# One program block instead of two, lists made earlier, and new instruction orders in a macaron layer of two expert blocks around attention

## The chip, the core and the metric

The kernel runs on one core of one Trainium2 chip. The core has five engines that run side by side and meet only at semaphores: TensorE (PE, matmuls and transposes; PEld is its weight load), VectorE (DVE), ScalarE (ACT), GpSimd (POOL) and SyncE (SP, which here only starts DMAs). Each engine works off its own list of instructions strictly in order. The metric is the device time of one launch in microseconds (us). Lower is better.

## What is computed

16 sequences of 256 tokens with 256 channels, all float32. The same expert block stands before and after attention, with the same weights:

```python
x = x + 0.5 * ffn(layernorm(x))
x = x + attention(layernorm(x))
x = x + 0.5 * ffn(layernorm(x))

def ffn(inp):                       # T = 4096 tokens, E = 32 experts, K = 4, F = 176, FS = 704
    x = w_norm * inp * rsqrt(mean(inp ** 2) + 1e-6)
    w_topk, sel = top_k(softmax(x @ w_router), 4)
    # per expert at most 128 slots: a token's place in its expert's list decides
    y = (silu(buf @ w_gate[e]) * (buf @ w_up[e])) @ w_down[e]
    out = scatter_add(y * w_topk)
    sh = silu(x @ sw_gate) * (x @ sw_up) @ sw_down
    return inp + out + sigmoid(x @ w_shared_gate) * sh
```

Attention has 16 query and 8 key heads of size 32, rotary positions, scores capped by a tanh and a causal softmax.

## The kernel before

The program has three stages, each a function that gives every engine its part: the first expert block (FFN1), attention, the second expert block (FFN2). `run` puts the stages one behind the other on each engine. The order of all work is the order of the code; no scheduler moves anything.

**Split numbers.** Dense products are made from a high and a low part of each operand, so each takes three matmuls (`split_matmul`, L85 to L89). A high part is a ScalarE copy (`high_gate_up`, `x_hi_parts`, `a_hi_part`), a low part a VectorE subtraction (`low_gate_up`, `x_lo_parts`, `a_lo_part`). The shared weights are split once, in FFN1: 12 pieces of gate and up, and then down.

**Expert block.** The 4096 tokens are 8 blocks of 512. For a block r: `statistics(r)` (VectorE), `scales(r)` (GpSimd), `make_z(r)` (ScalarE), `turn(r)` (TensorE transposes), `x_hi_parts`, `x_lo_parts`, `router(r)`, `take_logits`, `turn_logits`, `top_experts`, `count`, `take_counts`, `weigh`. The shared expert of a block is 11 chunks of gate and up (`chunk`, L87 to L89 with `gu`) and 4 down products (`down_proj`); `silu_of`, `product`, `a_hi_part`, `a_lo_part` and `outputs` stand between. Slots 0 to 3 do blocks 0 to 3 of the shared expert and route all 8 blocks beside them. Then come the lists: `tile_starts` (L841) and `list_bounds` (L1227 to L1230), `list_tiles` (L1235 to L1237), and for each of 8 groups of four experts `find` (L850) and `list_experts` (L1243 to L1250), which writes the slots that GpSimd's `gather` (L773) reads. In `lead` 18 pieces of the shared expert of block 4 stand between the lists. Behind it each of 32 experts takes a pass: `turn_rows` (L979), `copy_rows` (L1406), `gate_up_expert` (L988), `turn_products` (L997), `down_expert` (L1008), with two or three pieces of the shared expert in it.

**Setup.** `setup` makes constants and loads the router, in a program block of its own: its end is a barrier of all engines (L309), and SyncE goes there only when the three zero fills of padding rows (L326) have landed.

**Attention.** One slot for a sequence b: scores, values, denominators of b beside the projections and rotary work of b + 1 and the output of b - 1. `score_unit` (L1623) needs `roped` from GpSimd, `weighted_values` (L1639) needs the probabilities that GpSimd has masked (`causal`, L1805), `denominators` (L1655) need VectorE's `add_tiles` (L1875), the value projection needs VectorE's `turn` (L1865). The last slot and FFN2's first slot (`slot_behind`) are interleaved by hand, since they share banks.

## Time and profile before

| | us |
|---|---|
| median of 3 runs | 977.32 (975.83 to 978.03) |
| the profiled execution | 977.82 |
| its span, first to last instruction | 976.1 |
| busy: TensorE / VectorE / ScalarE / GpSimd | 915.5 / 692.2 / 531.6 / 503.1 |

Times in the profile count from the first instruction of the span. A line of the timeline gives start, length, engine, source line, operation and tiles, and in brackets how long the engine had been idle before and what it had waited for. FFN1 fills the span up to about 352 us, attention up to about 650, FFN2 the rest. The granted TensorE clock is given as a share of full speed; its two levels are 2.4 GHz (1.0) and 1.2 GHz (0.5).

### The profile page before, as it was taken

How to read it: one execution, taken by the hardware profiler on the slowest of the kernel's cores; microseconds unless marked ns; L12 is line 12 of the kernel's file. 1: busy time of each engine (PE TensorE's matmuls, PEld its weight loads, DVE VectorE, ACT ScalarE, POOL GpSimd, SP SyncE). 2: the span in 40 equal slices, each digit the busy share in tenths (PEclk: the TensorE clock that was granted, in tenths of full speed). 3: DMA queues.
4: the chain of work that ended last, by engine and by line, in shares of the span. 5: the costliest groups of instructions: out<-in, count | busy, mean ns of one | idle time of the engine just before them, and what ended most of it. 6: DMA issues, size and time to landing. Idle time of an engine off the chain costs nothing.

```text
span 976.1 us, 18320 instructions
## 1 busy us (share of the span) xinstructions
PE 915.5 (94%) x6274; PEld 686.8 (70%) x6274; DVE 692.2 (71%) x1704; ACT 531.6 (54%) x794; POOL 503.1 (52%) x536
## 2 busy tenths in 40 slices
PE   1999998999999999999999999888999989999997
PEld 1778886777778775666666666547888857777786
DVE  4888777644344677998998999987887685444445
ACT  3666762223233467888888788776666522332322
POOL 5341212455563277788788788752431125556530
PEclk9999999999999999999999999999999999999999
DMA  5333126577776520100100102003332167777735
GB/s 196 102 96 112 52 76 177 144 182 185 177 182 144 157 87 13 33 22 30 35 22 21 43 11 77 22 12 124 117 116 71 49 183 168 174 180 179 187 46 173
DMA packets 95434, 101.91 MB, mean 104 GB/s; under 512 B 18689, under 2 KB 86657, under 8 KB 95361
## 3 DMA queue, kind: packets, MB, share of 16 engines
q1 hardware_dynamic: 83072, 83.17, 27.9%
q0 software_dynamic: 12288, 17.83, 10.6%
q8 instruction: 37, 0.61, 0.3%
q14 instruction: 37, 0.30, 0.1%
HBM read 65.44 MB, written 35.54 MB: 103 GB/s over the span
## 4 chain that ended last, share of the span: by engine, by line
PE 42%; DVE 14%; issue 4%; ACT 4%; POOL 2%; DVEq 0%; POOLq 0%; ACTq 0%
PE zT L988 4%; PE gu L87 3%; PE gu L89 3%; PE gu L88 3%; PE pj_at L87 3%; PE gu L1008 3%; PE pv_at L1639 3%; PE pj_at L89 2%; PE pj_at L88 2%; PE scores_at L1623 2%; PE down L87 2%; PE down L89 2%; DVE turned_at L1865 2%; PE down L88 2%; PE den_at L1655 2%
## 5 line engine op out<-in xcount | busy, mean ns | idle before, releaser
L87 PE MATMUL gu<-x_hi,gu_hi 128*128 128x512 f32 x264 | 122.2, 463 | 4.8 <-DVE act_gu L1259 4.8
L773 POOL DMA_INDIRECT rows<-z_rows,slots x64 | 67.9, 1061 | 75.4 <-DVE slots L1250 56.4
L1730 ACT ACTIVATE capped_at<-scores_at 128x2048 f32<-128x2048 f32 x64 | 93.1, 1455 | 24.5 <-PE scores_at L1623 24.2
L1066 ACT CAST a_hi<-act_gu 128x512 fp32r<-128x512 f32 x96 | 59.1, 616 | 86.8 <-DVE act_gu L1259 74.2
L89 PE MATMUL gu<-x_lo,gu_hi 128*128 128x512 f32 x264 | 104.9, 398 | 0.0
L88 PE MATMUL gu<-x_hi,gu_lo 128*128 128x512 f32 x264 | 104.6, 396 | 0.0
L1738 ACT ACTIVATE probs_at<-capped_at 128x2048 f32<-128x2048 f32 x64 | 95.1, 1487 | 2.5
L87 PE MATMUL down<-down_hi,a_hi 128*128 128x256 f32 x300 | 94.5, 315 | 0.2 <-DVE a_lo L1269 0.2
L1805 POOL TENSOR_SCALAR_AFFINE_SELECT probs_at<-probs_at 128x1024 f32<-128x1024 f32 x64 | 85.8, 1344 | 16.7 <-ACT probs_at L1738 16.0
L1142 ACT ACTIVATE y<-gu,rows 128x256 f32<-128x256 f32 x64 | 30.3, 473 | 109.8 <-PE gu L1008 96.0
L988 PE MATMUL zT<-w_gu,xT 128*128 128x352 f32 x256 | 86.3, 460 | 0.0
L781 POOL DMA_INDIRECT out<-y,slots x32 | 50.9, 1592 | 68.4 <-DMA out<-y,slots 48.7
L781 POOL DMA_INDIRECT acc<-y,slots x32 | 50.8, 1587 | 66.8 <-DMA acc<-y,slots 50.6
L88 PE MATMUL down<-down_hi,a_lo 128*128 128x256 f32 x300 | 84.5, 282 | 0.0
L89 PE MATMUL down<-down_lo,a_hi 128*128 128x256 f32 x300 | 84.4, 281 | 0.0
L280 POOL TENSOR_TENSOR rstd_f<-var_in_f,neg_half 128x8 f32<-128x8 f32 x16 | 27.0, 1690 | 111.0 <-DVE var_in_f L274 111.0
L1406 DVE TENSOR_SCALAR xT<-zT,w_norm_pairs 128x128 f32<-128x128 f32 x128 | 39.0, 346 | 62.4 <-PE zT L979 62.4
L1058 ACT ACTIVATE silu<-gu 128x512 f32<-128x512 f32 x80 | 47.6, 594 | 57.0 <-PE gu L89 57.0
L1793 POOL TENSOR_TENSOR by_sin_at<-turned_at,sin 128x512 f32<-128x512 f32 x48 | 70.2, 1463 | 6.6 <-DVE turned_at L1865 6.6
L1798 POOL TENSOR_TENSOR roped_at<-by_cos_at,by_sin_at 128x512 f32<-128x512 f32 x48 | 71.9, 1498 | 2.6
L1008 PE MATMUL gu<-w_down,prodT 88*128 88x256 f32 x256 | 70.7, 399 | 0.6 <-issue 0.6
L1269 DVE TENSOR_TENSOR a_lo<-act_gu,a_hi 128x512 fp32r<-128x512 f32 x80 | 55.0, 688 | 18.9 <-ACT a_hi L1066 17.8
(250 smaller groups left out, 2596.4 us busy)
## 6 DMA issues: line engine op xcount, KB each, us to landing
w_gu<-in_w_gate SPq DMA_DIRECT2D x64, 176.0 KB, 2.4
w_gu<-in_w_up SPq DMA_DIRECT2D x64, 176.0 KB, 2.9
w_down<-in_w_down SPq DMA_DIRECT2D x64, 176.0 KB
z_rows<-z SPq DMA_DIRECT2D x16, 512.0 KB, 3.0
acc<-base SPq DMA_DIRECT2D x10, 512.0 KB, 3.3
out<-base SPq DMA_DIRECT2D x10, 512.0 KB, 3.4
xn_at<-acc SPq DMA_DIRECT2D x16, 256.0 KB, 2.7
x<-xn_at SPq DMA_DIRECT2D x16, 256.0 KB, 2.1
```

The lines of the kernel that those rows point to most:

```text
L87: nc.tensor.matmul(out, w_hi, x_hi, start=first, stop=False)
L88: nc.tensor.matmul(out, w_lo, x_hi, start=False, stop=False)
L89: return nc.tensor.matmul(out, w_hi, x_lo, start=False, stop=last)
L773: pool.indirect_dma_start(out=gathered_rows[:, n, :], out_offset=None, in_=m.z_rows, in_offset=bass.IndirectOffsetOnAxis(ap=slots[:, e:e + ...
L781: pool.indirect_dma_start(out=acc, out_offset=bass.IndirectOffsetOnAxis(ap=slots[:, e:e + 1], axis=0), in_=y[:, e % HELD_Y, :], in_offset= ...
L988: last = nc.tensor.matmul(gu_ps, xT[:, e % 2, k, :], w_gu[:, n, :, k, :], start=k == 0, stop=k == KC - 1)
L1008: last = nc.tensor.matmul(y_ps, prodT[:, e % 2, k, :], w_down[:, n, k, :], start=k == 0, stop=k == 1)
L1730: nc.scalar.activation(capped[:, u % 2, :, 0:n], scores[:, :, 0:n], ACT.Tanh, scale=QK_SCALE / SOFTCAP).then_inc(capped_ready, 1)
L1738: nc.scalar.activation(probs[:, u, :, 0:n], capped[:, u % 2, :, 0:n], ACT.Exp, scale=SOFTCAP).then_inc(exp_ready, 1)
L1793: pool.tensor_tensor(by_sin[:, n], turned[:, n], sin, ALU.mult).then_inc(sin_done, 1)
L1798: pool.tensor_tensor(roped[:, q, c:c + 2, :], by_cos[:, n], by_sin[:, n], ALU.add).then_inc(roped_ready, 1)
L1805: pool.affine_select(out=diag, in_=diag, compare_op=ALU.is_ge, fill=m.zero_reg, base=0, pattern=[[0, JH], [0, REP], [1, P]], channel_multi ...
```

## The change

1. **Setup** loses its own block. Its parts become the first instructions of each engine's only list. TensorE waits for the constants and, before `router(0)`, for the router's split; GpSimd waits for the zero fills ahead of the first gather.
2. **First rows.** `scales` writes z's shift ahead of the numbers that only the base needs, and two semaphores tell the two apart. `turn` transposes tile by tile as each tile of z arrives, `router` starts with the first half of the low part. Gate and up have a load semaphore each; the 12 splits run gate first, six ahead of `make_z(0)`, three behind it, three behind `x_hi_parts(0)`. The split of down goes from the middle of slot 0 to the time ahead of it, its high part on GpSimd ahead of `scales(1)`.
3. **Lists.** `tile_starts` goes ahead of the last down product of slot 3, `list_bounds` ahead of the second `outputs` and `list_tiles` behind it. In `lead` one list stands behind each product. Lists 4 to 7 come in passes 0, 2, 4, 6 instead of 0, 1, 2, 3. `take_counts` goes ahead of the last `a_lo_part`.
4. **Expert weights.** SyncE holds back the loads of experts 2 and 3 until the second gather has landed.
5. **Attention.** The split of the output weights goes from ScalarE and VectorE to GpSimd, behind its first slot. In the first slot `add_tiles` goes ahead of the third `turn`; in slots 14 and 15 and FFN2's first slot some instructions change places.

```diff
-        sp.dma_start(self.up[:], self.ins["sw_up"].rearrange("(k p) f -> p k f", p=P)).then_inc(self.gu_loaded, 16)
+        sp.dma_start(self.gate[:], self.ins["sw_gate"].rearrange("(k p) f -> p k f", p=P)).then_inc(self.gate_loaded, 16)
+
+    def load_up(self, sp):
+        sp.dma_start(self.up[:], self.ins["sw_up"].rearrange("(k p) f -> p k f", p=P)).then_inc(self.up_loaded, 16)
+
+    def load_down(self, sp):
         sp.dma_start(self.down[:, 0:MT - 1, :], self.ins["sw_down"][0:(MT - 1) * P, :].rearrange("(c p) n -> p c n", p=P)
...
-    def high_gate_up(self, act):
-        act.wait_ge(self.gu_loaded, 32)
-        for hi, lo, raw in self.gu_splits:
+    def high_gate_up(self, act, first, behind):
+        act.wait_ge(self.gate_loaded if behind <= MT else self.up_loaded, 16)
+        for hi, lo, raw in self.gu_splits[first:behind]:
             act.copy(hi, raw).then_inc(self.hi_made, 1)
 
     def high_down(self, pool):
         pool.wait_ge(self.down_loaded, 48)
         pool.tensor_copy(self.m.down_hi[:], self.down[:]).then_inc(self.down_hi_made, 1)
 
-    def low_gate_up(self, dve):
-
-        for n, (hi, lo, raw) in enumerate(self.gu_splits):
+    def low_gate_up(self, dve, first, behind):
+
+        for n in range(first, behind):
+            hi, lo, raw = self.gu_splits[n]
...
         pool.tensor_tensor(self.rstd[:, q], self.var_in[:, q], self.m.neg_half[:], ALU.pow).then_inc(self.rstd_ready, 1)
         pool.tensor_scalar(self.back[:, q], self.moments[:, q, :, 0], -1.0, None, ALU.mult)
         pool.wait_ge(self.rstd_ready, b + 1)
-        pool.tensor_tensor(self.z_scale[:, q], self.rstd[:, q, 0], self.rstd[:, q, 1], ALU.mult)
+        pool.tensor_tensor(self.z_scale[:, q], self.rstd[:, q, 0], self.rstd[:, q, 1], ALU.mult).then_inc(self.factors_ready, 1)
+        pool.wait_ge(self.factors_ready, 2 * b + 1)
+        pool.tensor_tensor(self.z_shift[:, q], self.back[:, q], self.z_scale[:, q], ALU.mult).then_inc(self.scales_ready, 1)
         pool.tensor_scalar(self.half[:, q], self.rstd[:, q, 0], 0.5, None, ALU.mult).then_inc(self.factors_ready, 1)
-        pool.wait_ge(self.factors_ready, b + 1)
-        pool.tensor_tensor(self.z_shift[:, q], self.back[:, q], self.z_scale[:, q], ALU.mult)
+        pool.wait_ge(self.factors_ready, 2 * b + 2)
         pool.tensor_tensor(self.base_shift[:, q], self.back[:, q], self.half[:, q], ALU.mult)
-        pool.tensor_scalar(self.base_scale[:, q], self.half[:, q], 1.0, None, ALU.add).then_inc(self.scales_ready, 1)
-
-
...
-        with nc.Block() as block:
...
-                sp.wait_ge(cleared, 3 * 16)
-                sp.wait_ge(loaded, (3 + KC) * 16)
...
+def setup(nc, m, ins, front, weights, scratch, sem):
...
+        front.load(sp, 0)
+        weights.load_gate(sp)
+        front.load(sp, 1)
+        weights.load_up(sp)
+        weights.load_down(sp)
+        sp.wait_ge(made, 2)
+        for rows in (m.z_rows, m.acc1, m.acc2):
+            sp.dma_start(rows[T:T + PAD, :], zeros[:, 0:rows.shape[1]]).then_inc(cleared, 16)
...
+    def on_tensor(pe):
+        pe.wait_ge(constants, 3)
+
+    def router_split(pe):
+
+        pe.wait_ge(router_made, 1)
+
+    def rows_cleared(pool):
+
+        pool.wait_ge(cleared, 3 * 16)
...
         def turn(r):
 
-            reached(pe, z_ready, TJ * (r + 1))
             at_least(pe, lT_taken, r)
-            for k in range(KC):
-                for j in range(TJ):
+            for j in range(TJ):
+                reached(pe, z_ready, TJ * r + j + 1)
+                for k in range(KC):
                     last = nc.tensor.transpose(zT[k][:, j * P:(j + 1) * P], z[:, r % 2, j, k * P:(k + 1) * P], m.ident[:])
-                last.then_inc(zT_ready, 1)
+                    if j == TJ - 1:
+                        last.then_inc(zT_ready, 1)
 
         def router(r):
 
-            reached(pe, lo_ready, KC * (r + 1))
             h = held(r)
             for k in range(KC):
+                reached(pe, lo_ready, KC * r + k + 1)
                 last = split_matmul(nc, zT[0][:], m.router_hi[:, k, :], m.router_lo[:, k, :], x_hi[h][:, k, :],
...
-            if not before:
+            if begin:
+                begin.on_sync(sp)
                 load_x(2)
...
             for e in range(HELD_W):
+                if e == 2:
+                    reached(sp, gathered[1], 16)
                 load_gate_up(e)
                 load_down(e)
...
+            if begin:
+                begin.on_gpsimd(pool)
             if before:
-                front.scales(pool, 2)
                 before.last_output(pool)
                 make_base(0)
                 make_base(1)
+                front.scales(pool, 2)
                 make_base(2)
             else:
                 make_base(0)
+                weights.high_down(pool)
                 front.scales(pool, 1)
                 make_base(1)
-                weights.high_down(pool)
                 front.scales(pool, 2)
                 make_base(2)
...
             for b in range(MERGED):
                 reached(pool, out_stored[held(b)], 16)
+            if begin:
+                begin.rows_cleared(pool)
...
                     if weights and b == 0:
-                        reached(pe, weights.lo_made, c + 1 if c < GU - 1 else weights.gu_total)
+                        reached(pe, weights.lo_made, MT + c // 2 + 1)
...
                 for j in range(TJ):
+                    if s is None and j == TJ - 1:
+                        tile_starts()
                     down_proj(b, j, range(MT))
...
             def lead():
-                tile_starts()
-                for p in range(0, 7):
+                for p in range(0, 6):
                     piece(p)
                 find(0)
                 find(1)
-                for p in range(7, 11):
+                for p in range(6, 10):
                     piece(p)
                 find(2)
-                for p in range(11, 13):
+                for p in range(10, 14):
                     piece(p)
                 find(3)
-                for p in range(13, LEAD):
+                for p in range(14, LEAD):
                     piece(p)
...
-                if e < 4:
-                    find(4 + e)
+                if e < 8 and e % 2 == 0:
+                    find(4 + e // 2)
...
+                begin.on_scalar(act)
+                weights.high_gate_up(act, 0, MT)
                 make_z(0)
+                weights.high_gate_up(act, MT, MT + 3)
                 x_hi_parts(0)
-                if weights:
-                    weights.high_gate_up(act)
+                weights.high_gate_up(act, MT + 3, 2 * MT)
                 take_logits(0)
                 make_z(1)
...
-                if weights and b == 0:
-                    weights.low_down(dve)
                 a_lo_part(b, 2)
                 product(b, 4)
                 a_lo_part(b, 3)
                 a_lo_part(b, 4)
                 product(b, 5)
+                take_counts(r)
                 a_lo_part(b, 5)
-                take_counts(r)
                 if s is not None:
                     statistics(s + 1)
                 outputs(b, 0)
...
                 if s is not None:
                     statistics(s + 2)
+                else:
+                    list_bounds()
                 outputs(b, 1)
+                if s is None:
+                    list_tiles()
...
             def slot_behind(f, r, s):
 
-                statistics(s)
                 before.vector_last_values(dve)
                 before.vector_last_low_part(dve)
                 product(0, 0)
                 top_experts(f)
                 before.vector_last_residual(dve)
+                statistics(s)
                 x_lo_parts(r)
...
             def lead():
-                list_bounds()
                 for p in range(0, 5):
                     followup(p)
-                list_tiles()
-                for p in range(5, 7):
+                list_experts(0)
+                for p in range(5, 9):
                     followup(p)
-                list_experts(0)
                 list_experts(1)
-                for p in range(7, 11):
+                for p in range(9, 13):
                     followup(p)
                 list_experts(2)
-                for p in range(11, 13):
+                for p in range(13, 17):
                     followup(p)
                 list_experts(3)
-                for p in range(13, LEAD):
-                    followup(p)
+                followup(17)
 
 ...
...
+                begin.on_vector(dve)
+                weights.low_gate_up(dve, 0, MT)
                 statistics(1)
+                weights.low_gate_up(dve, MT, MT + 3)
                 x_lo_parts(0)
-                if weights:
-                    weights.low_gate_up(dve)
+                weights.low_gate_up(dve, MT + 3, 2 * MT)
+                weights.low_down(dve)
                 slot(0, *ROUTES[0])
...
-            weighted_values(b, q, 0)
+            if ahead:
+                weighted_values(b, q, 0)
             score_unit(b, q, 2)
             if ahead:
                 project(b + 1, 1 - q, 2)
                 project(b + 1, 1 - q, 3, (1,))
+            else:
+                weighted_values(b, q, 0)
             weighted_values(b, q, 1)
             score_unit(b, q, 3)
...
-            elif not ahead:
+            cap(b, 2)
+            if not ahead:
                 act.wait_ge(roped_ready, (SEQS - 1) * PIECES + 2)
                 following.x_hi_parts(0)
-            cap(b, 2)
...
             causal(b, 1)
+            rope_sum(b + 1, 1 - q, 0)
             if following:
                 following.front.scales(pool, 0)
-            rope_sum(b + 1, 1 - q, 0)
-            if following:
                 causal(b, 2)
-                causal(b, 3)
             rope_sin(b + 1, 1)
             rope_sum(b + 1, 1 - q, 1)
             if not following:
                 causal(b, 2)
-                causal(b, 3)
+            causal(b, 3)
             rope_sin(b + 1, 2)
             rope_sum(b + 1, 1 - q, 2)
...
+            if not behind:
+                add_tiles(b, 0)
             turn(b + 1, 2)
             if behind:
                 y_lo_part(b - 1, 1)
-            add_tiles(b, 0)
+                add_tiles(b, 0)
...
+            y_lo_part(b - 1, 1)
+            take_values(b, 0, dve, dve.tensor_copy)
             dve.wait_ge(roped_ready, b * PIECES + 2)
             following.x_lo_parts(0)
-            y_lo_part(b - 1, 1)
-            take_values(b, 0, dve, dve.tensor_copy)
...
-            nc.scalar.copy(o_hi[:], m.o[:]).then_inc(o_hi_ready, 1)
...
             gpsimd_slot(0, 0)
+            pool.wait_ge(ffn_stored, 1)
+            pool.tensor_copy(o_hi[:], m.o[:]).then_inc(o_hi_ready, 1)
+            pool.wait_ge(o_hi_ready, 1)
+            pool.tensor_tensor(o_lo[:], m.o[:], o_hi[:].bitcast(F32), ALU.subtract).then_inc(o_lo_ready, 1)
...
-            dve.wait_ge(o_hi_ready, 1)
-            dve.tensor_tensor(o_lo[:], m.o[:], o_hi[:].bitcast(F32), ALU.subtract).then_inc(o_lo_ready, 1)
```

ScalarE, the first rows, before. `gu_hi` is the high part of the shared weights, `z` the first block's rows, `x_hi` its transposed high part; the two branches are the end of setup's block and the start of the main one.

```order
L361 CAST router_hi<-act_gu 128x256
L309 UNCONDITIONAL_BRANCH
L2193 UNCONDITIONAL_BRANCH
L617 ACTIVATE z<-x_f,z_shift_f,z_scale_f 128x256 x4
L627 ACTIVATE x_hi<-zT_1,w_norm 128x512 x2
L136 CAST gu_hi<-raw_gate 128x2x128
L136 CAST gu_hi<-raw_up 128x2x128
L136 CAST gu_hi<-raw_gate 128x2x128
```

The same place after the change:

```order
L355 CAST router_hi<-act_gu 128x256
L135 CAST gu_hi<-raw_gate 128x2x128 x5
L135 CAST gu_hi<-raw_gate 128x2x64
L627 ACTIVATE z<-x_f,z_shift_f,z_scale_f 128x256 x4
L135 CAST gu_hi<-raw_up 128x2x128 x3
L637 ACTIVATE x_hi<-zT_1,w_norm 128x512 x2
L135 CAST gu_hi<-raw_up 128x2x128 x2
L135 CAST gu_hi<-raw_up 128x2x64
```

The block's end is gone, and nine of the twelve splits stand ahead of `x_hi` instead of behind it.

VectorE, from the second outputs of slot 3 (`base_fourth`) to the first list (`slots`), before. `start` to `to_end` is `list_bounds`, `in_tile` to `rank` with `tile_f` is `list_tiles`, `act_gu` a product of the shared expert.

```order
L1288 SCALAR_TENSOR_TENSOR base_fourth<-down_1,half_gate,base_fourth 128x256 x2
L1227 TENSOR_SCALAR start<-small 128x8
L1228 TENSOR_TENSOR end<-small,rank 128x8
L1229 TENSOR_TENSOR in_tile<-slot_f,start 128x1024
L1230 TENSOR_TENSOR to_end<-slot_f,end 128x1024
L1259 TENSOR_TENSOR act_gu<-silu,gu_1 128x512
L1235 TENSOR_TENSOR in_tile<-in_tile,to_end 128x1024
L1236 TENSOR_TENSOR rank<-rank,start 128x1024
L1237 CAST rank<-tile_f 128x8
L1269 TENSOR_TENSOR a_lo<-act_gu,a_hi 128x512
L1243 TENSOR_SCALAR below<-small,part_f 128x508
L1244 TENSOR_SCALAR absent<-small,pad_f 128x4
```

After:

```order
L1249 TENSOR_SCALAR start<-small 128x8
L1250 TENSOR_TENSOR end<-small,rank 128x8
L1251 TENSOR_TENSOR in_tile<-slot_f,start 128x1024
L1252 TENSOR_TENSOR to_end<-slot_f,end 128x1024
L1310 SCALAR_TENSOR_TENSOR base_fourth<-down_1,half_gate,base_fourth 128x256 x2
L1257 TENSOR_TENSOR in_tile<-in_tile,to_end 128x1024
L1258 TENSOR_TENSOR rank<-rank,start 128x1024
L1259 CAST rank<-tile_f 128x8
L1281 TENSOR_TENSOR act_gu<-silu,gu_1 128x512
L1265 TENSOR_SCALAR below<-small,part_f 128x508
L1266 TENSOR_SCALAR absent<-small,pad_f 128x4
L1269 TENSOR_REDUCE local<-below 128x4
```

Both parts of the bounds now stand ahead of the first product, and the list follows the product at once.

GpSimd, the end of its first attention slot, before (`rstd_at` with `var_in_at` opens the next slot):

```order
L1793 TENSOR_TENSOR by_sin_at<-turned_at,sin 128x512
L1798 TENSOR_TENSOR roped_at<-by_cos_at,by_sin_at 128x512
L2102 UNCONDITIONAL_BRANCH
L2102 ISA
L76 REGISTER_ALU
L1784 TENSOR_TENSOR rstd_at<-var_in_at,neg_half 128x2
```

After:

```order
L1820 TENSOR_TENSOR by_sin_at<-turned_at,sin 128x512
L1825 TENSOR_TENSOR roped_at<-by_cos_at,by_sin_at 128x512
L2129 CAST o_hi_at<-o 128x1024
L2131 TENSOR_TENSOR o_lo_at<-o,o_hi_at 128x1024
L2132 UNCONDITIONAL_BRANCH
L2132 ISA
L76 REGISTER_ALU
L1811 TENSOR_TENSOR rstd_at<-var_in_at,neg_half 128x2
```

The two instructions on the output weights, which stood on ScalarE and VectorE, now stand between the slots of GpSimd.

## Rows read from the trace of the kernel before

**Rows 1.** The page, busy time of the engines: us, share of the span, instructions
```profile
PE 915.5 (94%) x6274; PEld 686.8 (70%) x6274; DVE 692.2 (71%) x1704; ACT 531.6 (54%) x794; POOL 503.1 (52%) x536
```

**Rows 2.** Waits of TensorE: who waited <- for whom: total us, times, longest
```profile
PE zT L599 <- ACT z L617: 18.8, 1, 18.8
PE gu L87 <- DVE act_gu L1259: 5.1, 5, 1.9
...
PE zT L997 <- DVE prod L1413: 2.9, 8, 0.7
PE pj_at L87 <- DVE turned_at L1865: 2.9, 5, 1.7
PE down L888 <- DVE a_hi L1272: 2.7, 3, 1.5
PE scores_at L1623 <- POOL roped_at L1798: 2.3, 1, 2.3
```

**Rows 3.** Timeline of the first 30 us, three engines: start, length, instruction
```profile
12.86 0.20 POOL L286 TENSOR_TENSOR z_shift_f<-back_f,z_scale_f 128x4 f32<-128x4 f32 x1
...
16.71 2.07 ACT L617 ACTIVATE z<-x_f,z_shift_f,z_scale_f 128x256 f32<-128x256 f32 x4 [11.27 <-PEq L309]
...
21.43 0.39 ACT L136 CAST gu_hi<-raw_gate 128x256 fp32r<-128x256 f32 x1
...
22.37 0.80 PE L87 MATMUL zT<-x_hi,router_hi 128*128 128x512 f32 x1 [1.56 <-DVE x_lo L632]
...
28.17 0.50 PE L87 MATMUL gu<-x_hi,gu_hi 128*128 128x512 f32 x1
```

**Rows 4.** Timeline of the SyncE queue, first 10 us: start, length of the issue
```profile
4.07 0.51 SPq L124 DMA_DIRECT2D raw_gate<-in_sw_gate  x1
...
9.05 0.43 SPq L326 DMA_DIRECT2D out<-zeros  x1
```

**Rows 5.** DMA issues of the first 62 us: count, size, us from issue to landing
```profile
raw_gate<-in_sw_gate SPq DMA_DIRECT2D x1, 704.0 KB, 5.4
...
out<-zeros SPq DMA_DIRECT2D x1, 128.0 KB, 7.2
```

**Rows 6.** Timeline of VectorE in slot 0
```profile
44.29 1.81 DVE L152 TENSOR_TENSOR down_lo<-raw_down,down_hi 128x1280 fp32r<-128x1280 f32 x2
```

**Rows 7.** Windows: length, busy us by engine, granted clock (PEclk), DMA share, GB/s
```profile
20.00:62.00 42.00, 38.49 (x218) 31.02 (x216) 35.24 (x120) 29.29 (x56) 18.86 (x35) 0.96 0.28 85
...
160.00:200.00 40.00, 37.48 (x201) 29.23 (x202) 25.90 (x69) 10.05 (x21) 18.23 (x15) 0.96 0.59 148
...
372.00:400.00 28.00, 26.30 (x233) 16.19 (x233) 23.55 (x46) 21.83 (x24) 19.86 (x20) 0.94 0.07 21
...
776.00:800.00 24.00, 19.40 (x102) 14.42 (x101) 18.73 (x44) 5.19 (x10) 6.21 (x6) 1.00 0.63 177
```

**Rows 8.** Timeline of FFN1 from the end of slot 3 to the first expert
```profile
149.28 0.88 DVE L1288 SCALAR_TENSOR_TENSOR base_fourth<-down,half_gate,base_fourth 128x256 f32<-128x256 f32 x2 [2.12 <-PE down L889]
...
157.52 0.74 DVE L1243 TENSOR_SCALAR below<-gu,part_f 128x508 bf16<-128x508 f32 x1
...
158.55 1.32 POOL L773 DMA_INDIRECT rows<-z_rows,slots  x1 [28.17 <-DVE slots L1250]
...
159.38 0.69 DVE L1259 TENSOR_TENSOR act_gu<-silu,gu 128x512 f32<-128x512 f32 x1
...
169.96 0.47 PE L979 MATMUL zT<-ident,rows 128*128 128x128 f32 x2 [1.26 <-DVE xT L1406]
```

**Rows 9.** Timeline of attention's first two slots
```profile
364.34 1.96 POOL L1805 TENSOR_SCALAR_AFFINE_SELECT probs_at<-probs_at 128x1024 f32<-128x1024 f32 x1
...
365.39 0.64 PE L1655 MATMUL den_at<-probs_at,ones_f 128*32 128x256 f32 x8 [1.60 <-DVE both_at L1875]
...
374.79 0.71 POOL L1784 TENSOR_TENSOR rstd_at<-var_in_at,neg_half 128x2 f32<-128x2 f32 x1 [4.26 <-DVE var_in_at L1852]
```

**Rows 10.** The page, a costly group: count | busy us, mean ns | idle before, releaser
```profile
L1793 POOL TENSOR_TENSOR by_sin_at<-turned_at,sin 128x512 f32<-128x512 f32 x48 | 70.2, 1463 | 6.6 <-DVE turned_at L1865 6.6
```

173 lines of the change are left out of this document (81 added, 92 removed).

## Prediction

> **What bounds the kernel now.** I read the busy times first, then TensorE's waits, then the timeline around each wait. TensorE is busy for 915.5 of 976.1 us [rows 1], so at most 60 us of idle time can be won, plus what its matmuls lose at the lower clock. Its waits are few and stand at a handful of places [rows 2]: 18.8 us before the first transpose, waits on VectorE's products, row copies and last low part in the expert blocks, and waits on VectorE and GpSimd at the two ends of attention. Between them TensorE runs without gaps, and time won ahead of such a stretch stays won if the other engines keep their lead. The change goes at those places. I price each by rebuilding the instruction order from the change's rows and the durations from the trace.
>
> **The setup's end.** GpSimd has written z's shift by 13.06 us, yet ScalarE begins z at 16.71 after waiting for the barrier [rows 3]. What held the barrier is the last zero fill, issued at 9.05 and 7.2 us on its way: 16.3 us [rows 4, 5]. Without the barrier, z waits for the shift alone, and the shift is written one instruction sooner: about 13.0 instead of 16.7, **3.7 us**. New on ScalarE ahead of z are six casts of gate, 0.39 us each, 2.3 us together [rows 3]; the gate weights land at 4.07 + 5.4 = 9.5 us [rows 4, 5], so the casts end at 11.8. Cost 0, or up to 0.5 if the load is later; I take 0.1. Three casts of up behind z cost 1.2 us on ScalarE, in the time in which it waited for the transposes: 0 to 0.5, I take 0.2. TensorE now transposes each tile as it comes and starts the router with the first half of the low part, where it waited 1.56 us for both halves [rows 3]: half of that, 0.8. Setup's sum: 3.7 - 0.1 - 0.2 + 0.8 = **4.2** (3.0 to 5.0). The router then starts near 18.2 us.
>
> The clock decides how much of this stays. The router's matmuls start at 22.37 at the lower level and the first at full speed is near 28.17 [rows 3]: 5.8 us after TensorE became busy for good. I expect the same distance again, so the gain is kept whole. The Trainium skill, page "TensorE: Matmul & The Clock Gate", section "Part 4: PE-mode transpose", says that transposes don't count as activity for the clock gate; by that rule the transposes that now begin earlier would bring nothing. The trace agrees as far as it can: the clock rose 5.8 us after the first matmuls and 9.3 after the first transposes. The sum is the same by the rule and by the row.
>
> **The split of down** took 1.81 us and a short copy in the middle of slot 0 [rows 6]. VectorE there runs without a break, and TensorE waited 1.5 us for its last low part just behind [rows 2] (the line of L888, its longest wait). With the split ahead of the slot, VectorE is 2.1 us earlier and that wait goes: **1.5**. What is late next is ScalarE's copy for the same part, which I place just ahead of TensorE. Behind that wait the clock fell: the window 20 to 62 has a mean of 0.96, that is 0.04 x 42 = 1.7 us of work lost [rows 7]. No wait of that size is left there, so I add **1.5** of the 1.7. Where the split stands now, VectorE waits for the router's logits anyway; GpSimd's high part ahead of `scales(1)` costs 1.5 us there, with z(1) wanted later by ScalarE: nothing. Sum 3.0 (1.5 to 3.2).
>
> **The lists.** Before, TensorE reached the second row turn at 169.96, waiting for VectorE [rows 8]; on its way it waited 1.9 for a product held up by two lists in a row [rows 2] (the line of L1259, once in each block) and lost 0.04 x 40 = 1.6 us to the clock [rows 7]. After, the chain is VectorE's own. The bounds fill its idle 2.12 us before the second outputs [rows 8] and push these from 149.3 to about 149.8; outputs and `list_tiles` end near 152.5. Then come, with no wait but 0.5 us for the first find, four lists at 1.86 us (157.52 to 159.38 [rows 8]) = 7.4, four products and four low parts at 0.6 = 4.8, and one row copy, 0.7. 152.5 + 0.5 + 7.4 + 4.8 + 0.7 = 165.9, so TensorE goes on **4.1 us** earlier. It will have reached the row turns near 163, so a wait of some 2.5 us stands there, more than the 1.3 now. In FFN2 the same program runs, but the clock is 1.00 over that stretch, 776 to 800 us [rows 7]: of FFN1's 1.6 I count 1 as part of the 4.1, so **3.1**. The two blocks: 7.2 (4 to 8.5). `tile_starts` one product earlier needs the ranks by then; `take_counts` ahead of the last low part starts that chain 1.4 us sooner, while VectorE waited for ScalarE: nothing.
>
> Lists 4 to 7 in every second pass take two of the waits on expert products away (2.9 us in 8 waits over both blocks [rows 2]) and may bring others: 0 to 2, I take **1.0**. Holding back the weights of experts 2 and 3 removes nothing from TensorE, since it never waited for rows; it keeps the earlier gather from queueing. Cost nothing, cover two expert passes. What it costs if the cover is gone is the last rival.
>
> **Attention's ends.** In the first slot the wait of 1.60 for `both_at` goes, but GpSimd's mask at 364.34 takes until 366.30, and the values behind the denominators need it [rows 9]: 0.1 to 0.9 is left. In the next slot TensorE waited 1.7 for a `turn` [rows 2] and the clock fell, 0.06 x 28 = 1.7 us [rows 7]; VectorE is freed of the low part of the output weights, and that wait shrinks. But GpSimd was idle for just 4.26 us before the slot [rows 9], and the split needs a subtraction of twice 512 elements, 2 x 1.46 = 2.9 [rows 10], and a cast, with one input instead of two, which I estimate at a third to half of it, 1.0 to 1.5: 3.9 to 4.4 of the 4.26. So the mask is late next, and the slot gains little: the sum is **0.5**, with -1.5 and +2.5 as ends. The last two slots reorder around a wait of 2.3 for `roped` [rows 2]; one mask of GpSimd no longer stands ahead of it. Behind it come the x_hi and x_lo parts, in the same order of engines as before, and the later `statistics` now delays x_lo of block 1: **0.5** (-1 to 2.3).
>
> **Sum.** 4.2 + 3.0 + 7.2 + 1.0 + 0.5 + 0.5 = 16.4 us. Against it stands the clock: it fell three times in the trace before, each time just behind a wait of 1.5 to 1.9 us, at some 1.7 us of work each [rows 2, 7], while FFN2's wait of the same 1.9 and the 2.3 for `roped` left it alone. Two or three waits of 2 to 2.5 us will be new, so I subtract **1.4**: 15.0. The profiled execution took 977.8, so 962.8; the median lies 0.5 below it, so **962.3**.
>
> **Rivals.**
> *Rows, not lists, set the lead.* GpSimd's first gather was issued at 158.55, and the second row turn came 11.4 us later [rows 8]. If that distance were needed, and not just there, the gather issued near 156.4 gives 167.8 and 2.1 us per block, 4.2 instead of 7.2: 965.3. Against it: TensorE has no wait on a gather.
> *The clock rises at the same instant as before.* From 18.2 to 28.2 us TensorE would run at the lower level, 10.0 us instead of 5.8, and lose half of the difference, 2.1: 964.4. For it: a single rise was seen, which can't tell an instant from a distance.
> *GpSimd and VectorE hold each other up over the output weights.* The mask of 1.96 us next to `both_at` [rows 9] shows that they do. If that makes the split half as long again, 6 us, the next slot's mask is 1.7 later than before: attention's start gives -1.5, 964.3. The Trainium skill, page "SBUF — State Buffer", section "Who interferes with whom", has a rule for it: a VectorE instruction with two inputs in SBUF and a GpSimd instruction that reads SBUF exclude each other for their whole length. By that rule, a subtraction of 2.9 us on GpSimd could stop `divide` or `add_tiles` for all of it, which is this rival's time.
> *Slower: the weights come too late.* SyncE waits for the second gather, and behind that wait stand the loads of all experts from 2 on. It decides from the point where these land later than TensorE's third pass, two passes behind 166. To undo 15 us and end above 979.3, both blocks would have to lose over 8.5 us each there; at 9 each, 980.3. Before, a gather landed within the 11.4 us above with all twelve loads in its way; now it has half of them. Hence small.
> *The change doesn't do what it says:* if any hidden order kept z at 16.7, setup would give 0.8: 965.7. The rows of the order speak against it.
>
> **How the numbers follow.** The forecast 0.60 (its own range 957.5 to 967); rows set the lead 0.10; the clock's rise 0.08; GpSimd and VectorE 0.12; z not earlier 0.02; slower 0.04; several small ones together, ending between 969 and 975, 0.04. The range takes the unknown ends: best case setup 5.0, split 3.2, lists 8.5, passes 1.5, attention 2 gives 20, so 957; at the other end the lists at 4, attention at -2 and a clock loss of 3 leave 8.5, so 969. About 0.18 lies outside. A measurement of this kernel can tell 0.2%, 2 us. Faster 0.95, same 0.01, slower 0.04.
>
> **What would show it.** In the profile after: z near 13.0 and the router near 18.2; full speed near 24; no wait at the last low part of slot 0 and a clock of 1.0 behind it; the second row turn 4.1 us closer to slot 3's last outputs, waiting for the row copy; the cast and the subtraction on GpSimd between 370 and 375 of the old count, with a wait of TensorE for a mask behind them; the weights of expert 2 issued after the second gather landed, and no wait for them. I would be wrong if the row turns wait for a gather, if the clock rises late, or if a wait for masks goes on beyond the second slot of attention.

## The result, and the profile after

The changed kernel takes 966.2 us (median of 4 runs, 964.96 to 966.7), the kernel before 977.67 us (4 runs, 975.83 to 978.88): a ratio of 0.9882, 95% interval 0.9863 to 0.9902. That is 11.5 us faster. The forecast was 962.3, 15.0 us faster. The measured time lies in the stated range, near its slow end, and 3.9 us above the forecast. The number alone would also fit the rival in which `z` comes no earlier (965.7); the rows below rule that out. The profiled execution took 965.7 us with a span of 964.0, against 977.8 and 976.1: 12.1 us of span.

The page answers to [rows 1]: TensorE is busy 2.1 us less, and its idle time fell from 60.6 us to 50.6.

```profile
PE 913.4 (95%) x6274; PEld 686.3 (71%) x6274; DVE 695.5 (72%) x1703; ACT 531.2 (55%) x793; POOL 511.1 (53%) x538
```

The waits of TensorE answer to [rows 2] (who waited <- for whom: total us, times, longest). The wait for `act_gu` in the lists and the wait of 1.5 for `a_hi` are gone. New is the 2.4 for `x_lo` in attention's last slot. The router's wait for `x_lo` grew from 1.6 to 3.0, and the waits for `xT`, the row copy, from 1.3 and 1.7 to 2.2 each.

```profile
PE zT L608 <- ACT z L627: 13.8, 1, 13.8
PE zT L997 <- DVE xT L1427: 4.4, 2, 2.2
PE pv_at L1663 <- POOL probs_at L1832: 4.4, 10, 1.6
PE zT L87 <- DVE x_lo L642: 3.7, 2, 3.0
PE pj_at L87 <- DVE turned_at L1890: 2.7, 4, 1.7
PE pj_at L87 <- DVE x_lo L642: 2.4, 1, 2.4
```

The start, as in [rows 3]. `z` begins at 13.05, as the sum had it. But the router waits until 18.90, since VectorE makes three low parts of `up` (2.64 us) ahead of `x_lo`. The last row is among the first matmuls at full speed.

```profile
13.05 2.08 ACT L627 ACTIVATE z<-x_f,z_shift_f,z_scale_f 128x256 f32<-128x256 f32 x4 [1.63 <-POOL z_shift_f L286]
15.45 2.64 DVE L146 TENSOR_TENSOR gu_lo<-raw_up,gu_hi 128x256 fp32r<-128x256 f32 x3 [0.37 <-ACT gu_hi L135]
16.18 1.64 POOL L139 CAST down_hi<-raw_down 128x1536 fp32r<-128x1536 f32 x1
18.02 1.40 DVE L642 SCALAR_TENSOR_TENSOR x_lo<-zT,w_norm,x_hi 128x512 fp32r<-128x512 f32 x2
18.90 0.76 PE L87 MATMUL zT<-x_hi,router_hi 128*128 128x512 f32 x1 [3.04 <-DVE x_lo L642]
24.53 0.50 PE L87 MATMUL gu<-x_hi,gu_hi 128*128 128x512 f32 x1
```

The windows answer to [rows 7] (length, busy us by engine, granted clock, DMA share, GB/s). Slot 0, the first expert block's passes and the first slots of attention, which had 0.96, 0.96 and 0.94, are at 1.00. In two other places the clock falls now.

```profile
20.00:60.00 40.00, 39.60 (x242) 32.31 (x241) 34.37 (x129) 27.07 (x47) 19.33 (x41) 1.00 0.35 105
160.00:200.00 40.00, 39.43 (x215) 30.57 (x213) 23.34 (x64) 9.47 (x22) 20.29 (x16) 1.00 0.68 166
360.00:388.00 28.00, 25.36 (x237) 16.03 (x236) 25.67 (x45) 22.06 (x24) 24.07 (x22) 1.00 0.06 20
620.00:640.00 20.00, 14.30 (x128) 7.96 (x128) 15.90 (x28) 13.20 (x12) 14.55 (x12) 0.91 0.01 4
780.00:800.00 20.00, 17.66 (x83) 13.13 (x83) 13.32 (x34) 5.16 (x11) 7.54 (x7) 0.91 0.60 164
```

A drop takes 0.09 x 20 = 1.8 us of the clock's work by these windows. What it delays is less, 0.9 to 1.5 us, as the comparison of kernels further down shows. Both drops follow a wait of over 2 us. The first line below is the wait ahead of the drop in FFN2 (at 158.80 in FFN1 the wait is 2.20 as well, and there the clock held), the other lines show the wait for `x_lo` in attention's last slot.

```profile
785.34 0.68 PE L997 MATMUL zT<-ident,rows 128*128 128x128 f32 x2 [2.22 <-DVE xT L1427]
```

```profile
630.48 1.25 ACT L637 ACTIVATE x_hi<-zT,w_norm 128x512 fp32r<-128x512 f32 x2
632.25 1.40 DVE L642 SCALAR_TENSOR_TENSOR x_lo<-zT,w_norm,x_hi 128x512 fp32r<-128x512 f32 x2
633.71 0.39 PE L87 MATMUL pj_at<-o_hi_at,y_hi_at 128*128 128x256 f32 x1 [2.36 <-DVE x_lo L642]
```

Since TensorE executes the same matmuls in almost the same order, the two traces can be laid on each other. The same matmul, before and after, gives the time won up to it:

| a matmul of TensorE | before | after | ahead | won in the stretch | forecast |
|---|---|---|---|---|---|
| first of the router | 22.37 | 18.90 | 3.47 | 3.5 | 4.2 |
| behind the last a_hi of slot 3 | 142.73 | 135.50 | 7.23 | 3.8 | 3.0 |
| second row turn, FFN1 | 169.96 | 158.80 | 11.16 | 3.9 | 4.1 |
| first Q/K projection of attention | 334.81 | 323.74 | 11.07 | -0.1 | 0.5 (passes) |
| output projection of slot 14 | 607.43 | 596.00 | 11.43 | 0.4 | 0.5 |
| chunk behind the wait for act_gu, first slot of FFN2 | 677.25 | 667.50 | 9.75 | -1.7 | 0.5 |
| behind the last a_hi of slot 3, FFN2 | 771.89 | 762.07 | 9.82 | 0.1 | 0 |
| second row turn, FFN2 | 798.17 | 785.34 | 12.83 | 3.0 | 3.1 |
| the end | 976.1 | 964.0 | 12.1 | -0.7 | 0.5 (passes) |
| clock, set apart | | | | | -1.4 |
| sum | | | | 12.1 | 15.0 |

What the experiments had to settle: why attention's end and the passes gave less than nothing, what the setup is held by now, whether lists or rows bound the lead, and how much a clock drop is worth, since the traces show it coming and going.

### The profile page after: what moved, and what is told of

It is laid out like the page before. It is cut to its first block, busy times and chain, and to the rows that moved or that the text cites. A ratio compares the mean times of both kernels' runs of the same rounds, so it can differ in the third digit from the quotient of the medians.

```text
span 964.0 us, 18310 instructions
## 1 busy us (share of the span) xinstructions
PE 913.4 (95%) x6274; PEld 686.3 (71%) x6274; DVE 695.5 (72%) x1703; ACT 531.2 (55%) x793; POOL 511.1 (53%) x538
## 4 chain that ended last, share of the span: by engine, by line
PE 46%; DVE 11%; issue 3%; POOL 3%; ACT 2%; DVEq 0%; POOLq 0%; ACTq 0%
PE zT L1006 4%; PE gu L87 4%; PE pj_at L87 4%; PE gu L89 4%; PE gu L88 4%; PE gu L1026 3%; PE pj_at L89 3%; PE pj_at L88 3%; PE pv_at L1663 3%; PE scores_at L1647 3%; PE down L87 2%; PE down L89 2%; PE down L88 2%; PE den_at L1679 2%; DVE turned_at L1890 2%
## 5 line engine op out<-in xcount | busy, mean ns | idle before, releaser
L1832 POOL TENSOR_SCALAR_AFFINE_SELECT probs_at<-probs_at 128x1024 f32<-128x1024 f32 x64 | 85.4, 1340 | 12.7 <-ACT probs_at L1765 12.1
```

Source lines behind the costliest of these rows:

```text
L1832: pool.affine_select(out=diag, in_=diag, compare_op=ALU.is_ge, fill=m.zero_reg, base=0, pattern=[[0, JH], [0, REP], [1, P]], channel_multi ...
```

## The experiments

The theory throughout is that each part acts in its own place and that the gains add, less what the clock takes; the rivals stand with each run. All times are medians of 4 runs beside 7 of the kernel before on the same chip (976.41 for the first four kernels, 977.24 for `z_held`, `down_back`, `outw_back` and `best_one`, 976.78 for the last four). The intervals are some 0.2% to either side, 2 us. The changed kernel stands at 966.2, but it was not timed beside these kernels; its ratio is 0.9882. So a difference of 1 or 2 us between two medians shows nothing by itself, and the readings below rest on the traces. Only the late lists and the kernels with several edits are clear of it. The runs are called, in the order below, `end_back`, `end_x_first`, `xlo_first`, `lists_late`, `z_held`, `down_back`, `outw_back`, `no_hold`, `passes_back`, and `best_one` to `best_three`.

### Attention's end put back

```diff
-            if ahead:
-                weighted_values(b, q, 0)
+            weighted_values(b, q, 0)
...
+            elif not ahead:
+                following.x_hi_parts(0)
             cap(b, 2)
-            if not ahead:
-                following.x_hi_parts(0)
...
+            following.x_lo_parts(0)
             y_lo_part(b - 1, 1)
             take_values(b, 0, dve, dve.tensor_copy)
-            following.x_lo_parts(0)
```

(also GpSimd's masks and scales of slot 14 and `statistics` in FFN2's first slot)

> The changed kernel with the orders of attention's last slots and of FFN2's first slot as they were before; all else as changed. Theory 1 (the new end of attention is what lost 1.7 us up to the first full expert slots of FFN2, and the clock drop at 635 us belongs to its wait of 2.36 for x_lo): the waits of 2.3, 2.0 and 1.4 us of before come back, the wait for x_lo and the clock drop there go, and the time is 1.0 to 2.0 us below the changed kernel's, near 964.7. Rival (the end was worth something, and FFN2 lost the time elsewhere): 966 to 968.

Measured: 966.0 us, ratio 0.9886 (0.9866 to 0.9905). The old waits are back (2.3, 2.0, 1.4), the one for `x_lo` is gone, but the clock fell here too.

```profile
625.35 1.14 PE L1647 MATMUL scores_at<-roped_at 32*128 32x512 f32 x8 [2.32 <-POOL roped_at L1822]
631.71 1.93 PE L1663 MATMUL pv_at<-probs_at,v_at 128*32 128x512 f32 x8 [1.97 <-POOL probs_at L1829]
637.38 0.71 PE L1647 MATMUL scores_at<-roped_at 32*128 32x256 f32 x8 [1.44 <-ACT capped_at L1754]
```

So neither side: the difference of 0.2 us is too small to tell, and from slot 14's output projection to the first full slot of FFN2 both traces, each with one drop, take the same time (71.6 and 71.5 us). TensorE's waits of over 0.2 us from 620 us to the first full slot of FFN2 sum to 8.6 us in the kernel before (the same stretch there) and 8.2 in the changed one. The -1.7 in the table is only in part the clock drop, which the execution before did not have. Kernels with the same orders and no drop there (`lists_late`, `z_held`) take 70.6 us for the stretch, the changed kernel 71.5, the kernel before 69.8. The drop took 0.9, and 0.8 is lost without it. Since `end_back` doesn't win it back, the new orders are not shown to be its cause; it stays open.

### x_hi and x_lo early in the last slot, the rest as changed

```diff
+            elif not ahead:
+                following.x_hi_parts(0)
             cap(b, 2)
-            if not ahead:
-                following.x_hi_parts(0)
...
+            following.x_lo_parts(0)
             y_lo_part(b - 1, 1)
             take_values(b, 0, dve, dve.tensor_copy)
-            following.x_lo_parts(0)
```

> The changed kernel, but in the last slot of attention ScalarE makes x_hi ahead of the cap of the third unit and VectorE makes x_lo ahead of the last y low part and the copy of values, as before. Theory 1 (these two moves alone made the new wait): the wait for x_lo falls from 2.36 to under 0.7, no clock drop at 635 us, the 1.3 us at roped stay won, and the time is 3 us below the changed kernel's, near 963. Rival (the third unit is then late, since its cap stands behind x_hi): a wait for capped or probs of 2 us or more takes the place, and the time is within 1 us of the changed kernel's, 965.5 to 967.

Measured: 965.15 us, 0.9879 (0.986 to 0.9897). The wait of 2.36 is gone and 1.02 for `capped` and 1.54 for the logits came for it; the waits of this stretch sum to 7.7 us, 0.5 less than in the changed kernel. The clock dropped four times in the profiled execution, one of them behind that 1.54. Neither theory fits in size: most of the wait of 2.36 comes back elsewhere.

### The first x_lo ahead of three low parts

```diff
-                weights.low_gate_up(dve, MT, MT + 3)
                 x_lo_parts(0)
+                weights.low_gate_up(dve, MT, MT + 3)
```

> The changed kernel, but VectorE makes the first x_lo ahead of three low parts of up. Theory 1 (TensorE's wait of 3.04 us ahead of the router is VectorE's 2.64 us on low parts): x_lo starts at 16.6 instead of 18.02, the router at 17.4 instead of 18.90, and the time is 1.5 us below the changed kernel's, near 964.7. On the clock: if it rises a fixed distance behind the first router matmul, full speed comes near 22.9; if at a fixed instant, it stays near 24.2 and about half of the gain is lost (965.5).

Measured: 964.9 us, 0.9884 (0.9864 to 0.9904), a ratio no better than the changed kernel's. The trace shows the gain:

```profile
16.66 1.41 DVE L642 SCALAR_TENSOR_TENSOR x_lo<-zT,w_norm,x_hi 128x512 fp32r<-128x512 f32 x2 [1.57 <-ACT x_hi L637]
17.56 0.77 PE L87 MATMUL zT<-x_hi,router_hi 128*128 128x512 f32 x1 [1.68 <-DVE x_lo L642]
```

The router is 1.34 us earlier and 1.9 are won at the second row turn of FFN1 (156.91), of which 0.5 come from an earlier rise of the clock. This is what my sum for the setup had missed: not the three casts on ScalarE, but their low parts on VectorE.

### Only two lists ahead of the experts

```diff
                 find(0)
                 find(1)
-                for p in range(6, 10):
-                    piece(p)
-                find(2)
-                for p in range(10, 14):
-                    piece(p)
-                find(3)
-                for p in range(14, LEAD):
-                    piece(p)
+                for p in range(6, LEAD - 1):
+                    piece(p)
+                turn_rows(0)
+                piece(LEAD - 1)
...
-                if e < 8 and e % 2 == 0:
-                    find(4 + e // 2)
+                if e < 12 and e % 2 == 0:
+                    find(2 + e // 2)
```

> The changed kernel, but only the first two lists are made ahead of the experts; lists 2 to 7 come in passes 0, 2, 4, 6, 8 and 10, all but one in one bank, and the first rows are turned one piece of the shared expert earlier. Theory 1 (the second row turn waits 2.2 us in each block for VectorE, which works on lists, not for rows): both waits go, the clock drop at 785 us too, and the time is 4.4 + 1.7 = 6 us below the changed kernel's, near 960. Rival (rows set the lead): the wait stays at 2 us and names a gather, and the time stays at 966.

Measured: 960.46 us, 0.9836 (0.9817 to 0.9855), 5.7 below the changed kernel. The wait of 2.2 is gone in both blocks; behind the 0.6 for slot 3's last `a_hi` no wait over 0.3 us stands until the end of the experts, and nobody waits for a gather. The two row turns of FFN1 (timeline) and the window of FFN2's lead (as above), where TensorE is busy for 29.71 of 30 us:

```profile
154.40 0.39 PE L993 MATMUL zT<-ident,rows 128*128 128x128 f32 x2
155.58 0.48 PE L993 MATMUL zT<-ident,rows 128*128 128x128 f32 x2
```

```profile
770.00:800.00 30.00, 29.71 (x154) 22.53 (x153) 20.54 (x52) 9.47 (x19) 14.66 (x12) 1.00 0.80 214
```

The rival that rows set the lead falls. Lists 2 and 3 are needed only by the gathers of experts 8 to 15, and the first of those goes out after the third expert's rows are added.

### z held until the zero fills have landed

```diff
                 weights.high_gate_up(act, 0, MT)
+                begin.rows_cleared(act)
                 make_z(0)
```

> The changed kernel, but ScalarE waits for the three zero fills ahead of the first z, as the barrier did; nothing else is undone. Theory 1 (what the old barrier held was the first z, and each us of it reached the end): the fills land near 16.3, z starts there instead of 13.05, the router at 22.1 instead of 18.90, and the time is 3.2 us above the changed kernel's, near 969.4; full speed comes near 27.5, as far behind the first router matmul as in the changed kernel. Rival (the lead of VectorE hides part of it further on): the loss is seen at the router, but is under 1.5 us at the second row turn, and the time is 966 to 968.

Measured: 966.97 us, 0.9893 (0.9877 to 0.991). `z` starts 3.4 us later, but the router only 2.0: VectorE's low parts of `up` are done beside that wait, and the 3.04 us shrink to 1.68.

```profile
16.43 2.08 ACT L627 ACTIVATE z<-x_f,z_shift_f,z_scale_f 128x256 f32<-128x256 f32 x4 [4.97 <-DMA out<-zeros]
20.93 0.77 PE L87 MATMUL zT<-x_hi,router_hi 128*128 128x512 f32 x1 [1.68 <-DVE x_lo L642]
```

The second row turn comes at 160.89, 2.1 later, so up to there the loss is kept whole, against the rival; and its size is 2.0, against my 3.2. With the changed order on VectorE the barrier's end was worth 2.0 of the 3.4 us that it released. The median shows only 0.8 us, inside the rival's range of time; how much is kept to the end is not shown.

### The low part of down back in slot 0

```diff
-                weights.low_down(dve)
                 slot(0, *ROUTES[0])
...
                 product(b, 3)
+                if weights and b == 0:
+                    weights.low_down(dve)
                 a_lo_part(b, 2)
```

> The changed kernel, but VectorE's low part of down stands in the middle of slot 0 again. Theory 1 (the wait at the last low part of slot 0 is this instruction's): a wait of 1.5 us for a_hi comes back near 47 to 48 us, the clock may fall behind it for another 1.7, and the time is 1.5 to 3.5 us above the changed kernel's, 967.7 to 969.7. Rival (take_counts ahead of the last low part and the setup's orders removed that wait): no wait over 0.7 us in slot 0, and the time is 966 to 967.

Measured: 967.27 us, 0.9894 (0.9877 to 0.991). The wait is back with the very length of [rows 2], and the clock falls behind it (12 us at 0.86 are 1.7 us).

```profile
48.33 0.38 PE L905 MATMUL down<-down_hi,a_hi 128*128 128x256 f32 x1 [1.47 <-DVE a_hi L1294]
```

```profile
46.00:58.00 12.00, 10.38 (x65) 9.79 (x65) 9.63 (x35) 7.30 (x14) 5.02 (x11) 0.86 0.15 47
```

In the profiled execution the second row turn is 4.1 us later than in the changed kernel's (162.87). The median shows 1.1 of it, under the 1.5 to 3.5 that I expected; the four executions lie between 966.2 and 969.0. The place is settled, the size only to within those 3 us.

### The output weights' split back on ScalarE and VectorE

```diff
             gpsimd_slot(0, 0)
-            pool.tensor_copy(o_hi[:], m.o[:])
-            pool.tensor_tensor(o_lo[:], m.o[:], o_hi[:].bitcast(F32), ALU.subtract)
...
             scalar_slot(0, 0, 2, behind=False)
+            nc.scalar.copy(o_hi[:], m.o[:])
...
             vector_slot(0)
+            dve.tensor_tensor(o_lo[:], m.o[:], o_hi[:].bitcast(F32), ALU.subtract)
```

> The changed kernel, but ScalarE and VectorE split the output weights behind attention's first slot again. Theory 1 (the split on GpSimd holds up VectorE: o_lo took 3.22 us, with both_at at 2.06 instead of 1.21 and var_in_at at 1.16 instead of 0.17; so nothing is gained by it): the waits of the second slot, now 0.51 + 1.70 + 0.37, sum to 2 to 3 us in the other order too, and the time is 965.5 to 967, no difference to be told. Rival (GpSimd was the right place): the wait for a turn grows by over 1 us and the time is above 967.

Measured: 963.92 us, 0.9869 (0.9853 to 0.9886). First the changed kernel, then this one:

```profile
359.93 2.06 DVE L1900 TENSOR_TENSOR both_at<-probs_at 128x1024 f32<-128x1024 f32 x1
360.99 3.22 POOL L2131 TENSOR_TENSOR o_lo_at<-o,o_hi_at 128x1024 fp32r<-128x1024 f32 x1
363.07 1.16 DVE L1877 TENSOR_SCALAR var_in_at<-moments_at 128x2 f32<-128x2 f32 x1
365.53 0.39 PE L87 MATMUL pj_at<-v_hi,aT_hi_at 128*128 128x256 f32 x1 [1.70 <-DVE turned_at L1890]
```

```profile
359.75 1.22 DVE L1900 TENSOR_TENSOR both_at<-probs_at 128x1024 f32<-128x1024 f32 x1
360.89 1.22 DVE L2140 TENSOR_TENSOR o_lo_at<-o,o_hi_at 128x1024 fp32r<-128x1024 f32 x1
364.66 0.39 PE L87 MATMUL pj_at<-v_hi,aT_hi_at 128*128 128x256 f32 x1 [1.60 <-DVE turned_at L1890]
```

From the third values of the first slot to the first of the second (two `pv_at` matmuls) it is 11.58 us with the split on GpSimd and 10.87 without: moving it cost 0.7 us. The median is 1.6 us below the range that I expected and 2.3 below the changed kernel; the profiled execution is 2.2 faster, of which 1.4 is the clock drop in FFN2 that it did not have. VectorE was to be freed of 1.2 us and lost 0.84 + 0.99 to GpSimd instead. This is the rival of the prediction in kind, though the late one is VectorE's `turn`, not the mask. The Trainium skill, page "SBUF — State Buffer", section "Who interferes with whom", has it that two-input instructions of VectorE and reads of GpSimd exclude each other; `both_at` agrees, 2.06 us against 1.22. `both_at` ran beside the cast of `o_hi_at` until 360.90, and the first 1.0 of the 3.22 us of `o_lo_at` lies beside it in turn. `var_in_at`, an instruction with one input, took 1.16 instead of 0.17 and ended with `o_lo_at` at 364.2. The sentence on two inputs does not cover it, but the same section names `tensor_scalar`, which it is, among the instructions that can take the shared ports with one input.

### The weights of experts 2 and 3 not held back

```diff
-                if e == 2:
-                    reached(sp, gathered[1], 16)
                 load_gate_up(e)
```

> The changed kernel, but SyncE no longer holds back the weights of experts 2 and 3 for the second gather. Theory 1 (the hold moves DMAs only, and TensorE waits neither for rows nor for weights): the same waits of TensorE, 2.2 us for VectorE's row copy in each block, and 965.5 to 967. Rival (the hold brings the first rows sooner, and part of the gain of the lists is its): a wait on a gather at the first or second row turn, and over 967.

Measured: 965.86 us, 0.9885 (0.9868 to 0.9902), the same time. But a wait on a gather is there now, hidden under VectorE's:

```profile
156.22 0.51 PE L995 MATMUL zT<-ident,rows 128*128 128x128 f32 x2 [0.63 <-DMA rows<-z_rows,slots]
158.04 0.47 PE L995 MATMUL zT<-ident,rows 128*128 128x128 f32 x2 [1.31 <-DVE xT L1425]
787.67 0.48 PE L995 MATMUL zT<-ident,rows 128*128 128x128 f32 x2 [2.21 <-DMA rows<-z_rows,slots]
```

At 787.67 the row copy ended only then as well (VectorE, 786.92 + 0.60), so the gather cost nothing. The hold gives nothing that can be told while VectorE is late. Whether it gives something with fewer lists in the lead was not tried.

### Lists 4 to 7 in passes 0 to 3

```diff
-                if e < 8 and e % 2 == 0:
-                    find(4 + e // 2)
+                if e < 4:
+                    find(4 + e)
```

> The changed kernel, but lists 4 to 7 come in passes 0 to 3 again. Theory 1 (a list beside a pass delays its product): the waits for prod at passes 1 to 3 of 0.7, 0.3 and 0.2 us come back, 1.0 to 1.2 in each block, and the time is 1 to 2 us above the changed kernel's, 967 to 968. Rival (they are hidden now, since the row copies run ahead): no such waits, 965.5 to 966.7.

Measured: 965.98 us, 0.9893 (0.9873 to 0.9913).

```profile
PE zT L1015 <- DVE prod L1434: 2.9, 8, 0.7
```

The waits are back as in [rows 2], yet the first projection of attention comes at 323.81, as in the changed kernel (323.74). From the second row turn to that projection it takes 164.8 us, as before the change. With the lists spread out, no drop and no wait at the block's end (`down_back`) it is 164.2, so the passes win 0.6 us in FFN1. In the changed kernel the end of the block took it: there TensorE waits for a load of the accumulated rows. In FFN2, from the second row turn to the end, it is 177.9 before and here, 177.2 in the six traces with spread lists and no drop, and 178.7 in the changed kernel, with one: 0.7 us won, and 1.4 lost to the drop. Three kernels, the end of the chain of scatter-adds on GpSimd and the VectorE instruction that reads the load behind it: the changed one, the one with x_lo first, and the one with attention's end put back. In this stretch all three have the same instructions.

```profile
309.60 1.65 POOL L794 DMA_INDIRECT acc<-y,slots  x1 [2.43 <-DMA acc<-y,slots]
316.32 0.75 DVE L1870 BATCH_NORM_STATS2 stats_at<-xn_at 128x6 f32<-128x256 f32 x2 [0.60 <-DMA xn_at<-acc]
```

```profile
305.58 1.57 POOL L794 DMA_INDIRECT acc<-y,slots  x1 [2.34 <-DMA acc<-y,slots]
315.00 0.75 DVE L1870 BATCH_NORM_STATS2 stats_at<-xn_at 128x6 f32<-128x256 f32 x2
```

```profile
311.82 1.56 POOL L794 DMA_INDIRECT acc<-y,slots  x1 [2.48 <-DMA acc<-y,slots]
318.22 0.75 DVE L1869 BATCH_NORM_STATS2 stats_at<-xn_at 128x6 f32<-128x256 f32 x2 [2.59 <-DMA xn_at<-acc]
```

Each of the 32 adds waits for the one before. The chain takes 141 to 147 us from its first to its last issue, 4.6 us an add; with the same instructions in this stretch the length differs from trace to trace. TensorE waited behind it 1.0 us, under 0.3 and 3.0 us in these three, and 0.3 us in the kernel before. Time won in FFN1 is therefore kept up to about the length of this chain, and what is won in the passes, behind the first add, is the part at risk.

### The best of them together

Best one is the late lists, the first x_lo first, and x_hi and x_lo early in the last slot. Best two adds the output weights' split on ScalarE and VectorE. Best three also masks the third unit earlier in attention's first slot:

```diff
             rope_sin(b + 1, 1)
+            if first:
+                causal(b, 2)
             rope_sum(b + 1, 1 - q, 1)
-            if not following:
+            if not following and not first:
                 causal(b, 2)
```

> The changed kernel with three edits together: only two lists ahead of the experts, the first x_lo ahead of the low parts of up, and x_hi and x_lo early in attention's last slot. Theory 1 (they act at different places, and their gains add): 5.7 us of the lists, 1.3 of the first x_lo and 1.0 of the last slot below the changed kernel's time, near 958.2. Rival (a lead won early is lost at a common later wait): 960 or more.

> Two lists ahead of the experts, the first x_lo ahead of the low parts of up, x_hi and x_lo early in attention's last slot, and the split of the output weights on ScalarE and VectorE as before the change. Theory 1 (the split on GpSimd costs 0.7 us in the second slot of attention: 11.6 us from its predecessor's third values to its own first values with it, 10.9 without): 0.7 us below the 957.5 of the version with the first three edits alone, 956.8. Rival (it comes back at the next wait): 957.5.

> The same four edits, and in attention's first slot GpSimd masks the third unit ahead of the second rotary sum. Theory 1 (TensorE's wait of 1.55 for that mask is one rotary sum of 1.28 us that stands ahead of it): the wait falls to 0.3 to 0.6, nobody waits for the rotary sum, and the time is 0.7 to 1.0 below that of the four edits, near 956. Rival (the sum is then late for the next scores): a wait for roped of 1 us or more, and no gain.

Measured: 957.54 us (0.9797, 0.9781 to 0.9814), 956.75 us (0.9793, 0.9776 to 0.9811) and 956.47 us (0.9794, 0.9776 to 0.9812). The first three gains add, and a little more (958.2 was expected). The three kernels cannot be told from each other; the mask's wait fell from 1.55 to 0.69, not quite to the 0.3 to 0.6 that I expected, 0.16 came back at the `turn`, and the median fell by 0.3 instead of 0.7 to 1.0. All three are some 9 us faster than the changed kernel. Of best three, the page and two windows:

```profile
PE 910.4 (95%) x6274; PEld 683.3 (72%) x6274; DVE 694.6 (73%) x1704; ACT 532.4 (56%) x794; POOL 505.0 (53%) x536
```

```profile
620.00:648.00 28.00, 22.85 (x187) 14.40 (x178) 22.95 (x57) 16.19 (x20) 11.60 (x18) 1.00 0.03 11
770.00:800.00 30.00, 29.61 (x156) 22.82 (x156) 19.71 (x50) 8.67 (x18) 17.08 (x14) 1.00 0.76 200
```

No wait behind the first matmul is over 1.9 us there, and no clock drop stands between the start and the last 15 us.

## Why the prediction held, and where it did not

**Setup, 4.2 forecast, 3.5 measured.** z came at 13.05 and the casts cost nothing, as worked out. The step that failed is "Three casts of up behind z cost 1.2 us on ScalarE", with its 0.2: it looked at ScalarE alone. On VectorE their low parts stand ahead of `x_lo` and took 2.64 us, one of the three 1.68 us long beside GpSimd's base and high part of down; before, every low part stood behind `x_lo`, and TensorE's wait for it was 1.56 [rows 3]. xlo_first gives 1.3 of it back, z_held shows that the barrier alone was 2.0. In z_held, where they run later, the same three low parts took 1.10 us.

**The clock's rise.** The distance was right: 24.53 - 18.90 = 5.6 us against 5.8 before, and in z_held, with the router 2.0 later, full speed came 2.2 later, at 27.07 against 24.87 (by the first two matmuls that start 0.23 us apart). The rival of a fixed instant falls: measured by those two matmuls, full speed came at 28.5 before and at 21.8 to 27.1 in the other thirteen traces. Yet the distance is no constant: so measured it is 6.0 us here, 6.1 before, and 3.5 to 6.3 us over the fourteen traces. That these two agree is luck. Among the kernels with the same orders up to slot 0, the first chunk behind the wait for `act_gu` near 41 us starts at 40.2 to 41.2. The Trainium skill, page "TensorE: Matmul & The Clock Gate", section "Part 4: PE-mode transpose", says that transposes don't count as activity; the traces don't contradict it, since the transposes began 5.1 us ahead of the router here and 3.5 before, and the rise came 6.0 and 6.1 behind the router. With the spread just given they can't show it.

**The split of down, 3.0 forecast, 3.8 measured.** Right in mechanism, wait and clock drop both gone; down_back brings both back.

**The lists, 4.1 and 3.1 forecast, 3.9 and 3.0 measured.** This chain of VectorE's durations was the best part: the wait of TensorE for the row copy, "some 2.5 us", is 2.2. Rows as the bound fell with lists_late.

**The passes, 1.0 forecast, -0.8 in the table.** The waits for `prod` did go, 2.9 us to 0.8, and by the traces without a drop or a wait at the block's end this is worth 0.6 + 0.7 = 1.3 us. The step that failed is that time won in a pass is kept: in FFN1 the chain of adds made TensorE wait 0.7 us longer than before (-0.1 in the table), in FFN2 a clock drop of 1.4 hid the gain (-0.7). I had not looked at what the end of the block waits for.

**Attention's start, 0.5 forecast, 0.4 measured,** for other reasons than those worked out. The waits grew by 0.9 us, and one clock drop went, which is worth 1.0 to 1.5 in this stretch by the kernels with and without one. The rival of GpSimd and VectorE holding each other up came in kind, not in size: the split took 4.8 us (1.50 + 3.22 and the gap), more than the 3.9 to 4.4 of the sum and less than the rival's 6, and cost 0.7 instead of 2.0; the mask of the third unit took the place of the wait for `both_at`, 1.55 for 1.60, since GpSimd's `by_sin` took 2.26 us beside `both_at`.

**Attention's end, 0.5 forecast, -1.7 measured.** The waits gained 0.4, the clock took 0.9, and the remaining 1.1 or 1.2 went in gaps of under 0.2 us that I did not follow. The prediction had "the x_hi and x_lo parts, in the same order of engines as before"; that is the step that can be named. `x_hi` stands behind a cap now and `x_lo` behind a copy, which made the wait of 2.36, with the clock drop behind it. The part in the gaps has no shown cause.

**The clock, -1.4 forecast.** I counted the three drops of before as gone, and less than one new, at 1.7 us, for two or three new waits of 2 to 2.5 us. The price was too high and the count too low. The same stretch of TensorE with the same orders, with and without a drop:

| from, to | without | with |
|---|---|---|
| second row turn of FFN1, first Q/K projection | 164.2 (down_back) | 165.5 (three kernels) |
| first Q/K projection, output projection of slot 14 | 272.2 to 272.3 (the changed kernel and three) | 273.3 to 273.8 (four) |
| output projection of slot 14, chunk behind `act_gu` | 70.6 (two) | 71.5 to 71.6 (the changed kernel and five) |
| second row turn of FFN2, the end | 177.2 (six) | 178.5 and 178.7 (two) |

A drop so delayed TensorE by 0.9 to 1.5 us. Counted over the traces of the changed kernel and its variants, one trace each, the clock fell behind the wait of 2.2 to 2.4 us at FFN1's second row turn in 4 of 9, at FFN2's in 2 of 9 and behind that for `x_lo` in 6 of 8: 12 of 26 (in one of the 9 the first is split into 0.63 and 1.31). That gives 1.3 x 4/9 + 1.4 x 2/9 + 0.9 x 6/8 = 1.6 us on average, near the 1.4 by luck; the profiled execution had two drops, 2.3. The clock is also one reason why the four executions of a kernel differ, by 1.2 to 3.6 us for the changed kernel and its nine variants: in the changed kernel the two with a mean clock of 0.996 took 965.0 and 965.7, the two at 0.992 and 0.993 took 966.7. It is not the only one, since the four of z_held, all at 0.996, lie 1.8 apart. Those of best one, at 0.999 to 1.000, lie within 0.6, those of best two and best three within 1.0 and 1.6.

**The slower rival** did not come: the loads of expert 2 were issued at 153.99, 3 us behind the second gather's issue, and TensorE waited for no weights.

The forecast missed 3.9 us of the median. By the profiled execution 2.9 are missing: 0.7 at the setup, 1.8 in the passes, 2.2 at attention's end and 0.4 in small ones, less 0.8 that down gave more, makes 4.3, of which 1.4 had been set apart for the clock. The last 1.0 is between profile and median: I took the median 0.5 below the profiled time, as before, and it is 0.5 above. That stays open.

## What to carry to other kernels

When an instruction is moved out of a critical chain on one engine, look at its partner on the next engine: the high parts cost nothing, their low parts cost 1.3 us. Price a new wait of TensorE with its length plus the chance of a clock drop, here about one in two for a wait over 2 us and 0.9 to 1.5 us each. And compare the same stretch over many traces before a loss is put down to the clock or to an order. And before making lists, loads or splits earlier, ask when each is first needed: two of four lists were not needed until three experts had been added, and leaving them out of the lead was worth 5.7 us, more than any other single edit here.

## What the hardware showed that I had not expected

- The clock drop is a matter of chance: five kernels that issue the same instructions up to FFN1's second row turn (the changed one, end_back, end_x_first, outw_back, passes_back) had the same wait of 2.2 us there. In two the clock fell to half speed behind it, in three it stayed at full speed.
- Two instructions can stretch each other, one behind the other: the addition of 1024 elements on VectorE took 2.06 us instead of 1.22, the subtraction of 1024 on GpSimd 3.22 with 1.0 of it beside that addition, and a VectorE instruction on 2 elements 1.16 instead of 0.17.
- An indirect add of 128 rows of 1 KB into HBM, each waiting for the last, has a period of 3.9 to 6.9 us. Thirty-two of them took 141 to 147 us in every trace, and nothing on TensorE shows this until its own work comes near that time.
